# A selective-scan kernel with the preparation of six of its eight tiles placed inside the scan steps

## Chip, cores and metric

One core of a Trainium2 chip. The metric is the device time of one launch in microseconds (us).

## The reference

Two layers on x of 4 batches x 1024 positions x 256 channels. The first, a selective scan with 32 states per channel, is where the change is:

```python
A = -jnp.exp(A_log)
deltaBC = jnp.einsum('bld,od->blo', x, W_bc)          # x: normalised input
dt_r, Bm, Cm = deltaBC[..., :64], deltaBC[..., 64:96], deltaBC[..., 96:]
dt = jnp.einsum('blr,dr->bld', dt_r, W_dt)
delta = jax.nn.softplus(dt + b_dt[None, None, :])
# for each position t:
#   h = exp(delta_t * A) * h + (delta_t * x_t) * B_t
#   y_t = sum over states of h * C_t
y = y + x * D_param
```

The second layer is a small attention-like block with top-1 routing; it takes layer norm of x + y, convolves, projects, routes and adds.

## The kernel before

Every engine runs its own program; semaphores order them. The 1024 positions are eight tiles of 128 (`LT`), and for the scan 32 chunks of 32 (`CHUNKS`). There are three stages.

Preparation goes over the eight tiles. SP loads x; VectorE takes mean and variance (`statistics`, L1483), GpSimd the reciprocal root (`rstds`), VectorE normalises (L1507), TensorE transposes (L1233) and multiplies: dt_r (L1242), C (L1251), B (L1257), dt (L1268). ScalarE makes softplus as Abs, Exp, Ln (L1397 to L1403), VectorE adds it up into delta (L1557) and multiplies du (L1560). delta is transposed on TensorE (L1218). GpSimd makes x + D*xn (L1112, L1117), stored as `base`. delta, du and B are each split into three bf16 parts whose products give fp32 accuracy; the parts go through DRAM scratch (`delta_terms`, `du_terms`, `b_terms`; stores at L974 and L1027), since the scan needs them in another layout. All DMAs are issued by SP, in program order.

The scan goes over chunks; a chunk has eight steps, two halves (`SUBS`) of 16 positions times four groups (`GROUPS`) of 64 channels. All 128 partitions hold 4 batches x 32 states. In one step TensorE makes the input term B*du in one of two pairs of PSUM banks (L1329), adds the carry of the half before (L1336), then makes the arguments delta*A of the next chunk (L1286, `decay_args`), and in every second step contracts finished states with C (L1298, `contract`). ScalarE takes their exponentials (L1429), GpSimd computes the carry (L1180) and zeroes its decay (L1183), and VectorE scans 1024 elements per partition (L1606). For a step G, TensorE waits for scan G-2 (`scan_done >= G-1`) and for carry G; the carry waits for scan G-4; VectorE waits for the input term and the decay of G; ScalarE may be two PSUM banks behind the arguments. SP loads the parts of the chunk after next: `load_md` (12 DMAs, L991) once the arguments of the present chunk are finished, `load_mu` (6 DMAs, L998 and L1002) once its input terms are. y leaves PSUM through ScalarE (L1436) from one of two banks.

The first scan waits (L1588 to L1590) for the stores of the delta parts of all tiles, and the scan of step 4 for all of preparation (`p_done`).

The third stage, routing, starts as the last scan ends and runs over eight tiles again (`phase_f_*`).

## Time and profile before

| | us |
|---|---|
| median of 3 runs | 1005.86 (1002.33 to 1007.05) |
| profiled execution | 1001.59 |
| its span | 999.9 |

| engine | busy us (share of the span) |
|---|---|
| TensorE (PE) | 873.0 (87%) |
| VectorE (DVE) | 831.2 (83%) |
| ScalarE (ACT) | 460.2 (46%) |
| GpSimd (POOL) | 395.3 (40%) |

The mean granted clock of TensorE is 0.903 of its 2.4 GHz. PEld is its weight load, SPq the queue of SP, with the time in which it issues DMAs. A share over the whole span mixes three stages with different limits, so a view of one stage has to be read for each.

### The profile page before, as it was taken

Reading aid. Unit: us, or ns where it says so; the run is one execution under the profiler, and the core shown is the slowest. Engines: PE = TensorE matmul, PEld = TensorE weight load, DVE = VectorE, ACT = ScalarE, POOL = GpSimd, SP = SyncE. Lnnn points to the kernel's source line nnn. Section 1 sums busy time; section 2 is a strip of 40 time slices with the busy share of each in tenths; the row PEclk is TensorE's granted clock in tenths of the full one; section 3 lists DMA queues with packets and bytes.
Section 4 is the critical chain, followed back from the end, with each engine's and each line's share of the span. In section 5 each row is a group of like instructions: output and inputs, shape, how many; then the busy total and the mean of one; then the engine's idle time right before and its main releaser. Section 6 shows DMA issues by size and latency. Waiting matters only on the chain.

```text
span 999.9 us, 22490 instructions
## 1 busy us (share of the span) xinstructions
PE 873.0 (87%) x7440; PEld 670.1 (67%) x7440; DVE 831.2 (83%) x861; ACT 460.2 (46%) x798; POOL 395.3 (40%) x737
## 2 busy tenths in 40 slices
PE   5666666159999999999999999999999969899994
PEld 3434444148777777777777777777777747787873
DVE  6655765307999999999999999999999976899884
ACT  1554444533454545544545545454545334443631
POOL 6253333412333333333333333333333544456434
PEclk9776555556999999999999999999999989999997
DMA  9399999392222222222222221222222334210101
GB/s 329 84 150 162 165 170 171 88 163 82 64 65 78 61 76 67 59 77 66 61 79 63 68 72 61 76 64 61 79 64 64 110 106 138 56 51 22 43 22 63
DMA packets 206072, 89.93 MB, mean 90 GB/s; under 512 B 139220, under 2 KB 191956, under 8 KB 205268
## 3 DMA queue, kind: packets, MB, share of 16 engines
q1 hardware_dynamic: 206036, 89.49, 38.1%
q8 instruction: 18, 0.29, 0.1%
q14 instruction: 18, 0.15, 0.0%
HBM read 45.85 MB, written 43.61 MB: 89 GB/s over the span
## 4 chain that ended last, share of the span: by engine, by line
PE 65%; SPq 16%; DVE 8%; POOL 4%; issue 3%; ACT 2%; DMA 1%; ACTq 0%; DVEq 0%; POOLq 0%
PE psum L1329 23%; PE psum L1298 13%; PE psum L1286 11%; PE psum L1336 9%; SPq L974 7%; SPq L1027 6%; PE psum L458 5%; POOL arena L399 2%; DVE arena L1606 2%; SPq L991 1%; POOL arena L390 1%; SPq L968 1%; PE psum L527 1%; DVE delta_mov L706 1%; ACT arena L564 1%
## 5 line engine op out<-in xcount | busy, mean ns | idle before, releaser
L1606 DVE TENSOR_TENSOR_SCAN arena<-arena,psum 128x1024 f32<-128x1024 f32 x256 | 570.9, 2274 | 48.4 <-DMA delta_terms<-arena 29.4
L1429 ACT ACTIVATE arena<-psum 128x512 f32<-128x512 f32 x512 | 278.0, 595 | 303.4 <-PE psum L1286 299.7
L1329 PEld LDWEIGHTS psum<-du_mov,b_sta 96*128 96x128 bf16 x2048 | 206.8, 131 | 130.2 <-DVE arena L1606 127.2
L1329 PE MATMUL psum<-du_mov,b_sta 96*128 96x128 bf16 x2048 | 273.0, 315 | 13.2 <-DVE arena L1606 13.1
L1180 POOL TENSOR_TENSOR carry<-arena 128x64 f32<-128x64 f32 x252 | 110.7, 439 | 357.0 <-DVE arena L1606 270.4
L1286 PE MATMUL psum<-delta_mov,a_sta 96*128 96x128 bf16 x2048 | 163.5, 224 | 8.3 <-ACT arena L1429 8.3
L1286 PEld LDWEIGHTS psum<-delta_mov,a_sta 96*128 96x128 bf16 x2048 | 144.1, 110 | 11.2 <-ACT arena L1429 10.7
L1336 PE MATMUL psum<-carry,ident 128*128 128x32 f32 x1024 | 149.2, 270 | 0.0
L1336 PEld LDWEIGHTS psum<-carry,ident 128*128 128x128 f32 x1024 | 148.4, 206 | 0.0
L1298 PE MATMUL psum<-arena,c_sta 128*32 128x512 f32 x1024 | 148.0, 643 | 0.0
L458 PE MATMUL psum<-delta_mov,arena 128*128 128x256 f32 (+6 forms) x544 | 114.6, 368 | 8.0 <-ACT arena L579 7.9
L458 PEld LDWEIGHTS psum<-delta_mov,arena 128*128 128x128 f32 x544 | 88.8, 194 | 29.7 <-ACT arena L579 9.8
L1183 POOL TENSOR_TENSOR arena<-zeros 128x64 f32<-128x64 f32 x256 | 76.5, 299 | 20.0
L1242 PE MATMUL psum<-arena 128*64 128x512 f32 x32 | 29.4, 1074 | 50.0 <-ACT arena L1377 50.0
L1135 POOL TENSOR_TENSOR arena<-c_sta,arena 128x1024 f32<-128x1024 f32 x8 | 18.6, 2324 | 77.0 <-ACT arena L1416 77.0
L1242 PEld LDWEIGHTS psum<-arena 128*64 128x64 f32 x32 | 6.0, 218 | 63.0 <-ACT arena L1377 53.0
L399 POOL TENSOR_TENSOR arena<-arena 128x768 f32<-128x768 f32 (+2 forms) x24 | 36.0, 1502 | 9.2 <-DVE arena L755 6.6
L390 POOL TENSOR_TENSOR arena<-arena,delta_mov 128x1024 f32<-128x1024 f32 x8 | 15.5, 1932 | 60.5 <-DVE delta_mov L814 60.5
L1557 DVE SCALAR_TENSOR_TENSOR arena<-psum,arena 128x1024 f32<-128x1024 f32 x8 | 9.8, 1224 | 33.2 <-ACT arena L1403 33.2
L1488 DVE BATCH_NORM_STATS2 arena<-arena 128x6 f32<-128x256 f32 x32 | 11.2, 412 | 29.4 <-DMA arena<-in_L_attn_x 29.3
L527 PE MATMUL psum<-delta_mov,arena 128*128 128x256 f32 x128 | 30.9, 397 | 2.8 <-ACT arena L621 2.8
L701 DVE TENSOR_TENSOR arena<-arena,psum 128x512 f32<-128x512 f32 (+3 forms) x32 | 14.3, 481 | 21.3 <-ACT delta_mov L595 11.6
(142 smaller groups left out, 819.7 us busy)
## 6 DMA issues: line engine op xcount, KB each, us to landing
du_terms<-arena SPq DMA_DIRECT2D x48, 256.0 KB, 3.9
du_mov<-du_terms SPq DMA_DIRECT2D x128, 96.0 KB
y<-y_rows SPq DMA_DIRECT2D x32, 256.0 KB
b_terms<-delta_mov SPq DMA_DIRECT2D x6, 1024.0 KB, 10.6
delta_terms<-arena SPq DMA_DIRECT2D x48, 128.0 KB, 5.3
delta_mov<-delta_terms SPq DMA_DIRECT2D x128, 48.0 KB
b_sta<-b_terms SPq DMA_DIRECT2D x64, 96.0 KB
arena<-in_L_attn_x SPq DMA_DIRECT2D x8, 512.0 KB, 5.3
```

Source lines behind the costliest of these rows:

```text
L399: pool.tensor_tensor(o[:, 0:n], o[:, 0:n], arena[:, AV_TMP[m]:AV_TMP[m] + n], ALU.add)\
L458: mm = nc.tensor.matmul(psum[:, at:at + n], xc, w_all[:, h * WCOLS + col:h * WCOLS + col + n], start=(h == 0), stop=(h == 1))
L974: sp_.dma_start(dram(scratch_d, s * per_term + offset, *dims_), part(which)).then_inc(count, 16)
L1027: sp_.dma_start(dram(delta_terms_d, s * (B * L * D) + lt * (B * P * D) + h * (P * TC), (TC, P), (TC * D, B * P // TC), (1, TC)), dp_view(k ...
L1180: ins = pool.tensor_tensor(carry[:, g, :], seg[:, :, 0], before[:, :, TS - 1], ALU.mult)
L1183: pool.tensor_tensor(seg[:, :, 0], zeros[:, :], zeros[:, :], ALU.add)\
L1286: mm = nc.tensor.matmul(psum[:, (4 + u % 2) * BANK + i * P:(4 + u % 2) * BANK + (i + 1) * P], a_sta[0:ROWS, dg * P:(dg + 1) * P], sub(delt ...
L1298: mm = nc.tensor.matmul(psum[32 * j:32 * j + 32, (6 + k) * BANK:(6 + k) * BANK + TP * D], c_sta[k][:, (pi * 4 + j) * 32:(pi * 4 + j + 1) * ...
L1329: mm = nc.tensor.matmul(sub(psum, 0, P, o, (4, 4), (TS, GD // 2)), b_sta[k][0:ROWS, (s * 4 + tg) * P:(s * 4 + tg + 1) * P], sub(du_mov[k], ...
L1336: mm = nc.tensor.matmul(sub(psum, 0, P, (pair_bank + half) * BANK, (TS, GD // 2)), ident[:, :], carry[:, g, half * (GD // 2):(half + 1) * ...
L1429: nc.scalar.activation(sub(arena, 0, P, k * CHUNK_ELEMS + u * 16 * TS, (TS, 16), (D * TS, SUBS), (1, TS)), sub(psum, 0, P, (4 + u % 2) * B ...
L1606: nc.vector.tensor_tensor_scan(state[s][:, seg], decay[k][:, (s * D + g * GD) * TS:(s * D + (g + 1) * GD) * TS], psum[:, 2 * (step % 2) * ...
```

## The change

- Tiles 0 and 1 are prepared ahead of the scan. Tile p = 2 to 7 is prepared during the scan of tile p-2 (`EARLY` = 2): after a step's own work, each engine's program calls `p_piece(p, n, first)`, n counting the 32 steps of a tile, which issues the pieces given to that step. The stores and the load of x are placed in SP's program by chunk.
- delta is made transposed. W_bc's part for dt_r and W_dt are multiplied once into `w_eff`, and z = w_eff * xn^T gives channels by positions, so dt_r, its copy and the transposes of delta go; du is made transposed and is transposed back (`du_transposes`), and B comes out of one product with C and a transpose. The maximum with zero becomes a Relu on ScalarE; sums, differences and products move from VectorE to GpSimd, and the casts to ScalarE, for the streamed tiles.
- The arguments of a chunk run two steps later (`AHEAD` = 2), and the first half's decay has one buffer instead of two, which makes room for a tile in preparation.
- y uses PSUM bank 6 alone and one row buffer; bank 7 serves preparation.
- The zero fill of `b_terms` is issued by ScalarE.

The core of the diff, added lines only; what they replace is in the functions printed above:

```diff
+EARLY = 2
+CT = 4
...
+        HALF_CHUNK = D * TS
+        DECAY_AT = (0, (HALF_CHUNK, 2 * HALF_CHUNK))
+        STATE_AT = (3 * HALF_CHUNK, 4 * HALF_CHUNK)
+        def decay_at(k, s):
+            return DECAY_AT[1][k] if s else DECAY_AT[0]
...
+        x_t = [slot(20), slot(8)]
+        xn = [slot(21), slot(9)]
+        xnT = [slot(22), slot(10)]
+        sp = [slot(23), slot(11)]
+        delta = [slot(24), slot(16)]
+        duT = sp
+        du = xn
+        base_tmp = [slot(13), slot(14)]
+        def half_slot(i, h):
+            return slot(i)[:, h * 512:(h + 1) * 512].bitcast(BF16)
+        dparts = [[half_slot(20, 0), half_slot(20, 1), half_slot(23, 1)],
+                  [half_slot(17, 0), half_slot(17, 1), half_slot(18, 0)]]
+        uparts = [[half_slot(22, 0), half_slot(22, 1), half_slot(23, 0)],
+                  [half_slot(19, 0), half_slot(19, 1), half_slot(18, 1)]]
...
@@ block.sync @@
+            store_base(0, 0)
+            store_base(1, 1)
+            sp_.wait_ge(S["b_filled"], 16 * 3)
+            store_b(0, 0)
+            sp_.wait_ge(S["first_parts"], FIRST["dlo"])
+            store_delta(0, 0)
+            sp_.wait_ge(S["zeros_ready"], 3)
+            sp_.wait_ge(terms_stored[0], 16 * (TERMS + D_STORES))
+            load_md(0, 0)
+            sp_.wait_ge(S["first_parts"], FIRST["ulo"])
+            store_du(0, 0)
+            load_md(0, 1)
+            sp_.wait_ge(terms_stored[0], 16 * STORES)
+            load_mu(0, 0)
+            sp_.wait_ge(S["du1_zeroed"], 1)
+            load_mu(1, 1)
+            store_b(1, 1)
+            sp_.wait_ge(S["dlo_ready"], 1)
+            store_delta(1, 1)
+            sp_.wait_ge(S["ulo_ready"], 1)
+            store_du(1, 1)
...
+            def m_tile(lt, first, stream, last):
+                p = lt + EARLY
+                if stream:
+                    settle(sp_)
+                    sp_.wait_ge(terms_stored[0], 16 * STORES * (p - 1))
+                    load_x(p, 0)
+                for kk in range(CT):
+                    c, k = CT * lt + kk, kk % 2
+                    if not (last and kk >= 2):
                         settle(sp_)
                         sp_.wait_ge(S["args_ready"], (c + 1) * UNITS)
+                        if kk == 2 and first:
+                            sp_.wait_ge(terms_stored[1], 16 * STORES)
+                        elif kk == 2:
+                            settle(sp_)
+                            sp_.wait_ge(terms_stored[0], 16 * STORES * (lt + 1))
+                        load_md(lt + (kk + 2) // CT, (kk + 2) % CT)
+                    if last and kk == 2:
+                        settle(sp_)
                         sp_.wait_ge(S["args_ready"], (c + 1) * UNITS)
                         load_f_weights(sp_)
+                    if last and kk == 3:
+                        settle(sp_)
                         sp_.wait_ge(S["b_ready"], c * STEPS)
+                        settle(sp_)
+                        sp_.wait_ge(S["y_stored"], 16 * 2 * CT)
                         f_load(sp_, 0, 0)
                         f_load(sp_, 1, 1)
+                    if stream and kk == 1:
+                        store_base(p, 0)
+                    if stream and kk == 3:
+                        settle(sp_)
+                        sp_.wait_ge(S["dlo_ready"], p)
+                        store_delta(p, 0)
+                    if not (first and kk == 0):
+                        store_y(c - 1)
+                    if stream and kk == 2:
+                        store_b(p, 0)
+                    if stream and kk == 3:
+                        settle(sp_)
+                        sp_.wait_ge(S["ulo_ready"], p)
+                        store_du(p, 0)
+                    if not (last and kk >= 2):
                         settle(sp_)
                         sp_.wait_ge(S["b_ready"], (c + 1) * STEPS)
                         load_mu(c + 2, k)
...
@@ block.gpsimd @@
+            rstds(0, 0)
+            rstds(1, 1)
+            for p in range(EARLY):
+                pool.wait_ge(S["first_xn"], p + 1)
+                base_product(p, p, base_tmp[p])
+                base_sum(p, p, base_tmp[p])
+            pool.memset(du_mov[1][:, :].bitcast(F32), 0.0).then_inc(S["du1_zeroed"], 1)
+            b_rest(0, 0)
+            b_low(0, 0)
             for k in range(2):
                 pool.memset(c_sta[k][:, :], 0.0).then_inc(S["c_sta_zeroed"], 1)
+            b_rest(1, 1)
+            b_low(1, 1)
+            delta_sum(1, 1)
+            du_product(1, 1)
+            delta_rest(1, 1)
+            delta_low(1, 1)
+            du_rest(1, 1)
+            du_low(1, 1)
             pool.wait_ge(S["c_sta_zeroed"], 2)
             pool.wait_ge(S["own_made"], 3)
...
+            def p_piece(p, n, first):
+                if n == 3:
+                    if first:
+                        pool.wait_ge(S["first_xn"], 2)
+                    else:
+                        pool.wait_ge(S["xn_ready"], p - 2)
+                    rstds(p, 0)
+                if n == 6:
+                    pool.wait_ge(S["xn_ready"], p - 1)
+                    pool.wait_ge(S["duT_psum"], 2 * p)
+                    pool.wait_ge(terms_stored[0], 16 * STORES * (p - 1))
+                    base_product(p, 0, sp[0])
+                if n == 8:
+                    base_sum(p, 0, sp[0])
+                if n == 18:
+                    b_rest(p, 0)
+                if n == 19:
+                    b_low(p, 0)
+                if n == 20:
+                    delta_sum(p, 0)
+                if n == 21:
+                    du_product(p, 0)
+                if n == 23:
+                    delta_rest(p, 0)
+                if n == 25:
+                    delta_low(p, 0)
+                if n == 27:
+                    du_rest(p, 0)
+                if n == 29:
+                    du_low(p, 0)
...
@@ block.tensor @@
+            def z_mul(k, half, at, o, n, h):
+                return nc.tensor.matmul(bank(at)[:, o:o + n], w_eff[:, h * D + half * P:h * D + (half + 1) * P],
+                                        xnT[k][:, h * BANK + o:h * BANK + o + n], start=(h == 0), stop=(h == 1))
+            def cb_products(k, at):
+                for o, w in ((0, R + N), (P, R)):
                     for b in range(B):
                         for h in range(2):
+                            mm = nc.tensor.matmul(bank(at)[N * b:N * b + N, o:o + P],
+                                                  w_bcT[:, h * P + w:h * P + w + N],
+                                                  xnT[k][:, h * BANK + b * P:h * BANK + (b + 1) * P],
                                                   start=(h == 0), stop=(h == 1))
+                mm.then_inc(S["bc_psum"], 1)
+            def p_piece(p, n, first):
+                if n == 6:
+                    pe.wait_ge(S["duT_taken"], 2 * p)
+                    pe.wait_ge(S["xn_ready"], p - 1)
+                    xn_transposes(0, 0, 7)
+                if n == 7:
+                    pe.wait_ge(S["xnT_ready"], 2 * p + 1)
+                    xn_transposes(0, 1, 7)
+                if 8 <= n < 16:
+                    half, i = (n - 8) // 4, n % 4
+                    if i == 0 and half == 0:
+                        pe.wait_ge(S["xnT_ready"], 2 * p + 2)
+                    if i == 0 and half == 1:
+                        pe.wait_ge(S["z_taken"], 2 * p + 1)
+                    mm = z_mul(0, half, 7, (i // 2) * D, D, i % 2)
+                    if i == 3:
+                        mm.then_inc(S["z_psum"], 1)
+                if n == 16:
+                    pe.wait_ge(S["z_taken"], 2 * p + 2)
+                    cb_products(0, 7)
+                if n == 17:
+                    b_transpose(p, 0, 7)
+                if n == 23:
+                    pe.wait_ge(S["bhi_ready"], p + 1)
+                    pe.wait_ge(S["du_ready"], p)
+                    du_transposes(0, 0, 7)
+                if n == 24:
+                    pe.wait_ge(S["duT_taken"], 2 * p + 1)
+                    du_transposes(0, 1, 7)
+            AHEAD = 2
...
+                            if step < AHEAD:
+                                for u in range((step + STEPS - AHEAD) * UNITS_PER_STEP,
+                                               (step + STEPS - AHEAD + 1) * UNITS_PER_STEP):
+                                    mm = decay_args(c, k, u, True)
+                            elif not (last and kk == 3):
+                                if step == AHEAD:
+                                    pe.wait_ge(md_loaded[1 - k], 16 * MD_LOADS * (2 * lt + (kk + 1) // 2 + 1))
+                                for u in range((step - AHEAD) * UNITS_PER_STEP, (step - AHEAD + 1) * UNITS_PER_STEP):
                                     mm = decay_args(c + 1, 1 - k, u, True)
+                            if stream:
+                                p_piece(lt + EARLY, kk * STEPS + step, first)
...
@@ block.scalar @@
+            act.wait_ge(S["zeros_ready"], 1)
+            row_elems = TERMS * B * L * P // P // 3
+            for i in range(3):
+                act.dma_start(dram(b_terms_d, i * P * row_elems, (row_elems, P), (1, row_elems)),
+                              delta_mov[0][:, 0:row_elems]).then_inc(S["b_filled"], 16)
...
+            def take_z(p, k, half, at):
+                act.wait_ge(S["z_psum"], 2 * p + half + 1)
+                cols = slice(half * BANK, (half + 1) * BANK)
+                nc.scalar.activation(sp[k][:, cols], bank(at), ACT.Abs, bias=bdt[:, half:half + 1])\
+                    .then_inc(S["z_abs"], 1)
+                nc.scalar.activation(delta[k][:, cols], bank(at), ACT.Relu, bias=bdt[:, half:half + 1])\
+                    .then_inc(S["z_taken"], 1)
+            def exp_part(p, k):
+                act.wait_ge(S["z_abs"], 2 * p + 2)
+                nc.scalar.activation(sp[k], sp[k], ACT.Exp, scale=-1.0).then_inc(S["sp_exp"], 1)
+            def ln_part(p, k):
+                act.wait_ge(S["sp_exp"], p + 1)
+                nc.scalar.activation(sp[k], sp[k], ACT.Ln, bias=1.0).then_inc(S["sp_ln"], 1)
...
+            def p_piece(p, n, first):
+                if n == 5:
+                    act.wait_ge(S["ulo_ready"], p - 1)
+                    if first:
+                        act.wait_ge(S["first_parts"], FIRST["ulo"])
+                    normalise(p)
+                if n == 6:
+                    act.wait_ge(terms_stored[0], 16 * STORES * (p - 1))
+                    take_xnT(p, 0, 0, 7)
+                if n == 7:
+                    take_xnT(p, 0, 1, 7)
+                if n == 11:
+                    act.wait_ge(S["base_ready"], p + 1)
+                    act.wait_ge(S["dlo_ready"], p - 1)
+                    take_z(p, 0, 0, 7)
+                if n == 15:
+                    take_z(p, 0, 1, 7)
+                if n == 16:
+                    exp_part(p, 0)
+                    take_cb(p, 0, 7)
+                if n == 17:
+                    act.wait_ge(S["blo_ready"], p)
+                    act.wait_ge(terms_stored[0], 16 * STORES * (p - 1))
+                    take_b(p, 0, 7)
+                if n == 18:
+                    b_middle(p, 0)
+                    ln_part(p, 0)
+                if n == 22:
+                    act.wait_ge(base_stored[0], 16 * p)
+                    delta_high(p, 0)
+                if n == 23:
+                    take_du(p, 0, 0, 7)
+                if n == 24:
+                    take_du(p, 0, 1, 7)
+                    delta_middle(p, 0)
+                if n == 26:
+                    du_high(p, 0)
+                if n == 28:
+                    du_middle(p, 0)
...
@@ block.vector @@
+            def p_piece(p, n, first):
+                if n == 2:
+                    dve.wait_ge(x_loaded[0], 16 * p)
+                    statistics(p, 0)
+                if n == 4:
+                    dve.wait_ge(S["rstd_ready"], p + 1)
+                    if not first:
+                        dve.wait_ge(S["xn_ready"], p - 2)
+                    nc.vector.scalar_tensor_tensor(out=shift, in0=mv[0][:, 0:7:2], scalar=-1.0, in1=rstd[0],
+                                                   op0=ALU.mult, op1=ALU.mult).then_inc(S["shift_ready"], 1)
```

## Rows read from the trace of the kernel before

**Rows 1.** Source view: count, duration ns min/median/max, first and last start

```profile
L1606 DVE TENSOR_TENSOR_SCAN arena<-arena,psum x256: 2260/2264/2289, 222.8 to 810.4; 128x1024 f32<-128x1024 f32 x128
```

**Rows 2.** Windows view, scan: busy us by engine, clock, DMA share, GB/s

```profile
222.80:812.70 589.90, 585.03 (x6033) 454.12 (x6033) 570.83 (x257) 282.59 (x524) 214.37 (x619) 0.98 0.24 72
```

**Rows 3.** Timeline, mid-scan: start, duration, engine, line, operation, idle before

```profile
503.02 18.04 DVE L1606 TENSOR_TENSOR_SCAN arena<-arena,psum 128x1024 f32<-128x1024 f32 x8 [0.23 <-PE psum L1336]
...
503.10 1.04 PE L1329 MATMUL psum<-du_mov,b_sta 96*128 96x128 bf16 x8
...
503.94 0.57 PE L1336 MATMUL psum<-carry,ident 128*128 128x32 f32 x4
...
504.77 1.09 ACT L1429 ACTIVATE arena<-psum 128x512 f32<-128x512 f32 x2 [0.60 <-PE psum L1286]
...
505.45 0.43 POOL L1180 TENSOR_TENSOR carry<-arena 128x64 f32<-128x64 f32 x1 [1.68 <-DVE arena L1606]
...
507.64 1.04 PE L1329 MATMUL psum<-du_mov,b_sta 96*128 96x128 bf16 x8
```

**Rows 4.** Timeline of SP's queue in preparation, issue times of groups of DMAs

```profile
11.64 10.59 SPq L960 DMA_DIRECT2D a_terms<-arena  x6
...
71.98 2.96 SPq L968 DMA_DIRECT2D a_sta<-a_terms  x4
75.47 7.41 SPq L1027 DMA_DIRECT2D delta_terms<-arena  x6
82.99 5.17 SPq L974 DMA_DIRECT2D du_terms<-arena  x6
...
178.00 7.81 SPq L991 DMA_DIRECT2D delta_mov<-delta_terms  x12
```

**Rows 5.** Timeline of SP's queue in the middle of the scan

```profile
500.09 1.81 SPq L998 DMA_DIRECT2D du_mov<-du_terms  x4
502.08 1.56 SPq L1002 DMA_DIRECT2D b_sta<-b_terms  x2
503.93 8.88 SPq L991 DMA_DIRECT2D delta_mov<-delta_terms  x12
```

**Rows 6.** DMA view: issues by destination, KB each, median us to landing

```profile
arena<-in_L_attn_x SPq DMA_DIRECT2D x8, 512.0 KB, 5.3
```

**Rows 7.** Timeline, TensorE: narrow products (preparation), transposes, fp32 products (routing)

```profile
54.25 0.70 PE L1251 MATMUL psum<-arena 128*32 128x128 f32 x16
...
888.35 1.04 PE L451 MATMUL psum<-ident,arena 128*128 128x128 f32 x8
889.31 3.69 PE L458 MATMUL psum<-delta_mov,arena 128*128 128x256 f32 x16
```

**Rows 8.** Timeline, routing stage: statistics of a tile, then the power

```profile
812.63 1.38 DVE L671 BATCH_NORM_STATS2 delta_mov<-arena 128x6 f32<-128x256 f32 x4
...
814.71 1.02 POOL L384 TENSOR_TENSOR delta_mov<-delta_mov 128x4 f32<-128x4 f32 x1 [4.46 <-DVE delta_mov L679]
```

**Rows 9.** Timeline: long operations of GpSimd and ScalarE, and one normalisation

```profile
156.75 2.12 POOL L1138 TENSOR_TENSOR arena<-arena 128x1024 bf16<-128x1024 f32 x1 [1.16 <-ACT arena L1418]
...
158.83 2.35 POOL L1112 TENSOR_TENSOR arena<-arena 128x1024 f32<-128x1024 f32 x1
...
160.95 1.28 ACT L1403 ACT_TABLE_LOAD   x1
...
162.24 1.06 ACT L1403 ACTIVATE arena<-arena 128x1024 f32<-128x1024 f32 x1
...
826.85 2.06 ACT L564 ACTIVATE arena<-arena,delta_mov 128x256 f32<-128x256 f32 x4
```

**Rows 10.** Windows view: the first scans, and around a pause of TensorE

```profile
227.80:240.80 13.00, 13.00 (x80) 11.14 (x78) 9.15 (x4) 4.34 (x8) 3.69 (x12) 0.50 0.17 57
816.00:820.00 4.00, 1.16 (x8) 0.86 (x8) 3.25 (x13) 3.25 (x6) 0.52 (x1) 0.87 0.26 52
824.00:828.00 4.00, 4.00 (x18) 3.04 (x18) 0.00 (x0) 1.65 (x4) 0.88 (x1) 0.77 0.73 218
```

838 lines of the change are left out of this document (378 added, 460 removed).

## The prediction

> **What bounds the kernel now.** I read the source view of the scan first [rows 1]: 256 instructions of one length, 2.26 us, the first at 222.8, the last ended at 812.7. So preparation of all eight tiles takes 222.8 us, the scan 589.9 and the routing stage the rest of the span, 187.2. Busy time within the scan [rows 2] puts TensorE at 585, VectorE at 571. Then comes one stretch of the timeline in the middle of the scan [rows 3]. Eight scans run without a gap in 18.04 us, after 0.23 us of waiting for L1336: 2.284 us a step. TensorE is not slack beside this. From one product B at L1329 (503.10) to the next but one (507.64) is 4.54 us, and two scans are 4.53 us; within it each operation starts as the one before ends. So both engines are full: work added to either lengthens a step, and a stall on either is kept. ScalarE and GpSimd have time over (283 and 214 us busy of 590, [rows 2]), but they have results due inside a step.
>
> I call S the start of B of a step. By [rows 3] the carry is wanted at S+0.8, and the exponentials end at S+2.8 (504.77 + 1.09 - 503.10).
>
> **Before the first scan.** The new kernel prepares two tiles instead of eight; SP's queue sets the end. Its stores of the split A are issued from 11.6 [rows 4]; the fill of b_terms, now on ScalarE's queue, still moves the same 6.3 MB beside them, so I take them as landed at 24 (bounds 18 and 28). Sixteen loads of a_sta, four in 2.96: 36. Tile 0's base store lands 5.3 after its issue, as x does [rows 6], and the split of delta, which writes over that tile, follows (four operations over 1024 columns, 1.06 each as Ln [rows 9]: 4): 45. Six delta stores 7.4, landed 4 later; twelve loads of delta_mov 7.8; du stores 5.2; twelve more loads 7.8: 77 [rows 4]. du_mov and b_sta 3.4 [rows 5], landing 4, gaps 0.8, B and carry at half clock 2.9: first scan at 88 (80 to 98) instead of 222.8. That is 135 us gained.
>
> Behind it SP issues load_mu(1) 3.4, b 5.2, delta 7.4, du 5.2, and only then load_x(2), landing 5.3 later: x of tile 2 is there at 108. VectorE asks for it in its third step, at 88 + 3 x 3.25 = 98, and cannot scan on.
>
> **A tile with preparation in it: what moves with it.** TensorE gets, per tile, 16 fp32 transposes at 0.12 (eight in 0.96, from 888.35 to 889.31): 1.9; eight z products of 256 columns, 3.53 (889.31 to 892.84); 16 small C and B products, twice the 0.70 of the eight at L1251, less a tail: 1.3; one transpose 0.1. Together 6.9 [rows 7], on a full engine. VectorE gets statistics, 2.0 (812.63 to 814.63), and the 0.2 of shift [rows 8].
>
> SP gets the stores, 5.2 + 7.4 + 5.2 + 1.7. In each tile's last chunk they stand in one line with the next load_x. From S of step 25: arguments finished 1.8, load_md 8.9, delta stores 7.4, y 0.7 as one of those loads, du stores 5.2, load_mu 3.4, gaps 0.6, x landing 5.3 [rows 4 to 6] = 33.3. The code puts it so: load_x(p) waits for the stores of p-1 and stands behind load_mu. VectorE asks for x behind step 2 of the next tile, which without waits is S25 + 9 x 2.284 + 3.9 = 24.5 later (28.2 with those of the carry below). So scans stop for 5 to 9 us in every streamed tile, queued behind `wait_ge(x_loaded[0])`. Bounds of the landing: 4 (an idle queue, the first x of the run) and 10 (the 128 x 16 x 6 pieces of 64 B of the delta stores still draining).
>
> After x: statistics 2.0, a scan 2.3, 0.1, then step 5 begins: 4.4. Twenty steps to step 25: 45.7. Onto these come the 6.9 of matmul work and the waits inside steps:
> - Step 6: normalise on ScalarE starts after the exponentials of step 5 and takes 2.06 [rows 9]; TensorE wants its transposes 0.4 earlier. GpSimd's base_product (2.35) then comes before the carry of step 7: 1.5.
> - Step 18: Ln needs a table load of 1.28 and the exponentials another, since here both loaded [rows 9]; with Ln 1.06 the arguments of step 20 wait 1.3.
> - Steps 22 to 30: a cast on ScalarE of 1.06, as Ln (till S+3.9), a GpSimd operation of 2.1 (S+6.1), the next carry 0.43: S+6.6 where S+5.4 is wanted. Less the 0.5 of a transpose group: 0.7 for step 24. The later three (3.7 together) lie inside the SP leg and cost nothing there, except in the last streamed tile.
> Sum 3.9, bounds 0 and 7 (the trace has no such queueing; the nearest is GpSimd waiting for ScalarE's cast in preparation, and I take the middle since each wait follows from durations in rows).
> - The clock. TensorE is idle for about 7 us at each x wait. In [rows 10] a stretch of 4 us with 1.16 busy ended with the clock falling to half, and in the 4 us around 825, after TensorE took up steady work at 822.9, it averaged 0.77; beside the first scans it stayed at half through 13 us of unbroken work. I take 2.0 per tile (0 to 5).
>
> The y bank costs nothing: its copy has from the contraction of step 3 to that of step 5. If ScalarE were late there, the contraction would wait; its lead is 2 us. The folded weight removes the dtr product and its copy from preparation, which is off SP's line.
>
> Streamed tile: 33.3 + 4.4 + 45.7 + 6.9 + 3.9 + 2.0 = 96.2, where a plain one is 73.1.
>
> **The sum.** S25 of tile 0 at 108.3 + 4.4 + 45.7 + 12.8 + 2 (half clock at the start) = 173.2. x of the next at 206.5. Four more tiles: 591.3. To the last S25: + 62.9 = 654.2. Seven steps and the three carry waits 19.7; 64 plain steps 146.2; last scan's end 2.1: 822.2. Routing stage as before, 187.2: 1009.4. Around the span lie 1.7 (1001.59 against 999.9): 1011. That is 9 us above the profiled execution's own time, and 5 above the median 1005.86 of the runs (the profiled one was 4 below it). So the 135 us come back: 138 in six tiles of 23 each, and some 10 at the first x.
>
> **Where the skill speaks.** The Trainium skill, page "ScalarE: Activation LUTs", section "Table sets: the hidden batching unit", says exp and ln share one set, so that ln after exp needs no second load. The trace disagrees: 1.28 us at L1403 ahead of Ln, and as much ahead of Exp. By the page step 18 would cost nothing and the sum be 8 us lower. On the clock, the Trainium skill, page "TensorE: Matmul & The Clock Gate", section "HAM oscillation — how this bites in real kernels", says that a wait for a DMA in every loop turn makes every turn start cold. The trace agrees for one wait [rows 10]; with that in each tile it is the second rival.
>
> **Rivals.**
> 1. The added work costs only itself. GpSimd, ScalarE and the clock have room; x still comes late. For it: steps are regular to 1%, and leads may absorb the waits. Against: results are due within one step. 1011 - 6 x 5.9 - 3.7 = 972. If x is in time from tile 1 on as well (SP's issue far faster than in preparation), each tile adds only 9.1: 88 + 589.9 + 9.8 + 54.6 + 187.2 + 1.7 = 931.
> 2. Slower. TensorE stays at half clock after every x wait. A step is 3.25 us then (four scans in 13 us at 0.50, [rows 10]). [...] 17 us of it is 5.2 steps x 0.97 = 5.1, and with the doubled transposes 6: 4 more per tile, 1035. A landing of 10 instead of 5.3 adds up to 24 more.
> 3. The change doesn't do what it says: the first scan is not early, since step 4 also waits for the stores of tile 1. Those land near 106, x at 108, so it is hidden; if the first scans came at 120, all shifts by 32: 1043.
>
> **Chances.** Forecast 0.42, rival 1 0.34 (972: 0.26; 931: 0.08), rival 2 0.20, rival 3 0.04. The likeliest case by itself spans 990 to 1025 (first scan, waits). Range: 948 to 1046, with the upper bounds of landing and the middle between the two forms of rival 1. A difference of 0.5% (5 us) is about what a measurement can tell from no change. Faster by over that, below 1000.8: rival 1 and a quarter of the forecast, 0.44. Within: 0.17. Slower: 0.39.
>
> **What would show it.** In the profile after: first scan at 88; VectorE waiting for the x load at step 2 in six tiles, 5 to 10 us each; clock below 1 right after; GpSimd's carry late for L1336 by 1 us behind base_product and the splits; SP busy in one line in each tile's last chunk; streamed tiles of 96 us, the last two of 73. No wait for x, or full clock throughout, and the number is wrong towards fast; scan steps of 3.25 us for long stretches, towards slow.

## The result, and the profile after

The changed kernel takes 1032.0 us (median of 4 runs, 1025.0 to 1035.3) against 1004.1 for the kernel before (999.96 to 1007.05): ratio 1.027, 95% interval 1.020 to 1.034. It is slower. The profiled execution took 1035.3 us, its span is 1033.4. The forecast was 1011 in a range of 948 to 1046, so the range held it and the forecast was 21 us low. Runs over 1.5% above the fastest of the same kernel are left out below: one of ten of the kernel with both edits, and two of four of the one with only TensorE's loop written out.

The page of the changed kernel: the span, the busy time by engine, TensorE's granted clock in 40 slices (9 is full), and the packets of the instruction queue.

```profile
span 1033.4 us, 21756 instructions
...
PE 886.0 (86%) x7468; PEld 677.4 (66%) x7468; DVE 763.5 (74%) x772; ACT 490.3 (47%) x883; POOL 456.7 (44%) x779
...
PEclk9655699899969896999699969899999998999998
...
q8 instruction: 69, 1.13, 0.5%
```

TensorE's clock is no longer full in the middle of the run; before it was, there (0.98 over the whole scan, first steps included, [rows 2]). The last row counts fetches of instructions: 69 packets, where the same row of the kernel before has 18.

VectorE's timeline in tile 0 (start, duration, what ended the idle time):

```profile
78.90 2.29 DVE L1736 TENSOR_TENSOR_SCAN arena<-arena,psum 128x1024 f32<-128x1024 f32 x1 [29.25 <-PE psum L1401]
...
98.61 1.41 DVE L1642 BATCH_NORM_STATS2 small<-arena 128x6 f32<-128x256 f32 x4 [10.95 <-DMA arena<-in_L_attn_x]
```

The first scan begins at 78.9 instead of 222.8 [rows 1]. After three steps VectorE stands 10.95 us for x. In tile 1 it stands again:

```profile
200.37 1.41 DVE L1642 BATCH_NORM_STATS2 small<-arena 128x6 f32<-128x256 f32 x4 [4.38 <-DMA arena<-in_L_attn_x]
```

SyncE's queue ahead of that second wait, from the arguments of step 25 on, which answers to the sum of [rows 4, 5]:

```profile
169.91 4.04 SPq L959 DMA_DIRECT2D delta_mov<-delta_terms  x12
174.06 7.32 SPq L944 DMA_DIRECT2D delta_terms<-arena  x6
...
183.57 6.34 SPq L951 DMA_DIRECT2D du_terms<-arena  x6
...
194.31 0.42 SPq L900 DMA_DIRECT2D arena<-in_L_attn_x  x1
```

The line is the forecast one, from delta_mov's load to delta's stores, du's stores and, last, x. Step 25 begins at 168.0, and x is there at 200.4: 32.4 us for a predicted 33.3. That the sum fits so well is partly luck: inside it the load of delta_mov was issued in 4.0 us (8.9 forecast), and du's stores in 6.3 (5.2), x's landing in 6.1 (5.3) and the gaps made up for most of it.

Then the forecast stops holding. In tiles 2 to 5 nobody waits for x. All engines at the seam between tiles 1 and 2:

```profile
283.06 1.13 PE L1333 MATMUL psum<-arena,c_sta 128*32 128x512 f32 x8
...
284.25 0.43 POOL L1204 TENSOR_TENSOR carry<-arena 128x64 f32<-128x64 f32 x1 [0.36 <-ACT arena L1547]
...
289.44 1.89 PE L1394 MATMUL psum<-du_mov,b_sta 96*128 96x128 bf16 x8 [5.25 <-issue]
...
292.23 2.29 DVE L1736 TENSOR_TENSOR_SCAN arena<-arena,psum 128x1024 f32<-128x1024 f32 x1 [6.66 <-PE psum L1401]
...
293.32 0.40 SPq L900 DMA_DIRECT2D arena<-in_L_attn_x  x1
```

TensorE's contraction at 283.06 belongs to step 31, and GpSimd has run ahead with the carries of the next steps, up to 284.25. TensorE starts B of step 0 (L1394) at 289.44, after 5.25 us released by "issue": no semaphore event explains it. VectorE waits 6.66 us behind it, and x, issued at 293.3, then comes in time for step 2. The same stop stands at 394.1 (5.10), 497.1 (5.00) and 600.3 (5.61). It is absent before tile 1, entered from straight code, and before tile 6, behind the loop. It is where the loop (`Fori`) over tiles 1 to 5 jumps back. TensorE's clock there, in stretches of 4 us (busy time of each engine, then PEclk, DMA share, GB/s):

```profile
core 0: us, PE busy (x) PEld busy (x) DVE busy (x) ACT busy (x) POOL busy (x), PEclk, DMA share, GB/s
284.00:288.00 4.00, 0.19 (x4) 0.00 (x0) 1.57 (x1) 0.03 (x1) 0.73 (x2) 0.79 0.86 235
288.00:292.00 4.00, 2.56 (x14) 2.56 (x15) 0.00 (x0) 0.00 (x0) 0.00 (x0) 0.50 0.77 217
292.00:296.00 4.00, 4.00 (x29) 3.86 (x26) 2.90 (x2) 1.34 (x3) 0.00 (x0) 0.50 0.56 177
296.00:300.00 4.00, 4.00 (x21) 2.28 (x19) 1.67 (x1) 0.83 (x2) 0.73 (x2) 0.51 0.33 101
300.00:304.00 4.00, 4.00 (x44) 2.94 (x44) 3.58 (x5) 2.49 (x5) 0.00 (x0) 1.00 0.13 37
...
308.00:312.00 4.00, 4.00 (x26) 2.75 (x24) 3.17 (x3) 1.83 (x5) 0.01 (x1) 0.50 0.12 46
```

The clock falls to 0.5 in the stop (the lower of its two levels, 1.2 of 2.4 GHz), stays there until 300 though TensorE is busy from 289.4 on, and is at 0.5 again from 308, after TensorE had waited 1.6 us for a carry. Behind the four jumps TensorE worked at half clock for some 10, 18, 18 and 10 us.

From the waits view (us in total, times, longest):

```profile
DVE arena L1736 <- PE psum L1401: 180.2, 98, 29.3
...
PE psum L1401 <- POOL carry L1204: 45.0, 33, 11.2
```

TensorE's longest stops for a carry stand where VectorE waits for x: 11.2 us in tile 0, 6.1 in tile 1, where the next carry stands on GpSimd behind the power for 1/std.

From statistics to statistics a tile lasts 101.8 us, then 102.3, 104.9, 102.9 and 103.0: 103.0 on average, where 96.2 was forecast.

### The profile page after: what moved, and what is told of

It reads as the page before. It is cut to its first block, busy times and chain, and to the rows that moved or that the text cites. A ratio compares the mean times of both kernels' runs of the same rounds, so it can differ in the third digit from the quotient of the medians.

```text
span 1033.4 us, 21756 instructions
## 1 busy us (share of the span) xinstructions
PE 886.0 (86%) x7468; PEld 677.4 (66%) x7468; DVE 763.5 (74%) x772; ACT 490.3 (47%) x883; POOL 456.7 (44%) x779
## 4 chain that ended last, share of the span: by engine, by line
PE 51%; issue 18%; DVE 9%; POOL 7%; ACT 6%; SPq 6%; DMA 2%; ACTq 0%; POOLq 0%; DVEq 0%
PE psum L1394 16%; PE psum L1333 9%; PE psum L1321 8%; PE psum L1401 8%; PE psum L427 5%; DVE arena L1736 3%; PE psum L1254 2%; POOL arena L368 2%; POOL carry L1204 2%; ACT arena L1547 1%; SPq L944 1%; POOL arena L359 1%; SPq L923 1%; PE psum L496 1%; ACT arena L1456 1%
## 5 line engine op out<-in xcount | busy, mean ns | idle before, releaser
L1394 PEld LDWEIGHTS psum<-du_mov,b_sta 96*128 96x128 bf16 x2048 | 226.4, 139 | 160.0 <-issue 89.4
L1394 PE MATMUL psum<-du_mov,b_sta 96*128 96x128 bf16 x2048 | 294.8, 333 | 29.5 <-issue 21.0
L1401 PE MATMUL psum<-carry,ident 128*128 128x32 f32 x1024 | 159.5, 281 | 45.0 <-POOL carry L1204 45.0
L1321 PE MATMUL psum<-delta_mov,a_sta 96*128 96x128 bf16 x2048 | 173.5, 232 | 17.5 <-ACT arena L1547 10.7
L1321 PEld LDWEIGHTS psum<-delta_mov,a_sta 96*128 96x128 bf16 x2048 | 153.0, 115 | 21.6 <-ACT arena L1547 14.2
L1333 PE MATMUL psum<-arena,c_sta 128*32 128x512 f32 x1024 | 157.2, 684 | 0.0
L427 PEld LDWEIGHTS psum<-delta_mov,arena 128*128 128x128 f32 x544 | 88.6, 194 | 29.6 <-ACT arena L548 9.5
L1254 PE MATMUL psum<-arena,w_eff 128*128 128x256 f32 (+1 forms) x112 | 43.2, 478 | 2.1 <-ACT arena L1462 2.1
L1333 PEld LDWEIGHTS psum<-arena,c_sta 128*32 128x32 f32 x1024 | 21.0, 112 | 21.3 <-issue 13.3
L1077 POOL TENSOR_TENSOR arena<-arena,d_bc 128x1024 f32<-128x1024 f32 x8 | 18.9, 2358 | 35.5 <-ACT arena L1456 34.6
L670 DVE TENSOR_TENSOR arena<-arena,psum 128x512 f32<-128x512 f32 (+3 forms) x32 | 14.3, 481 | 21.6 <-ACT delta_mov L564 11.9
L496 PEld LDWEIGHTS psum<-delta_mov,arena 128*128 128x128 f32 x128 | 25.5, 201 | 7.2 <-ACT arena L590 3.4
```

The costliest lines, as they stand in the source:

```text
L427: mm = nc.tensor.matmul(psum[:, at:at + n], xc, w_all[:, h * WCOLS + col:h * WCOLS + col + n], start=(h == 0), stop=(h == 1))
L496: mm = nc.tensor.matmul(psum[:, 6 * BANK + b * D:6 * BANK + (b + 1) * D], fgT[:, (h * B + b) * P:(h * B + b + 1) * P], w_out[:, h * D:(h + ...
L1254: return nc.tensor.matmul(bank(at)[:, o:o + n], w_eff[:, h * D + half * P:h * D + (half + 1) * P], xnT[k][:, h * BANK + o:h * BANK + o + n ...
L1321: mm = nc.tensor.matmul(psum[:, (4 + u % 2) * BANK + i * P:(4 + u % 2) * BANK + (i + 1) * P], a_sta[0:ROWS, dg * P:(dg + 1) * P], sub(delt ...
L1333: mm = nc.tensor.matmul(psum[32 * j:32 * j + 32, 6 * BANK:6 * BANK + TP * D], c_sta[k][:, (pi * 4 + j) * 32:(pi * 4 + j + 1) * 32], sub(ar ...
L1394: mm = nc.tensor.matmul(sub(psum, 0, P, o, (4, 4), (TS, GD // 2)), b_sta[k][0:ROWS, (s * 4 + tg) * P:(s * 4 + tg + 1) * P], sub(du_mov[k], ...
```

## The experiments

Theory B is the prediction's: SyncE's line to x and the waits inside the steps set a tile. Theory A: the jump of the loop costs by itself. Theory D came after the first results: short stops of TensorE cost twice, by the half clock behind them. Experiments 1 to 4, 5 to 8 and 9 to 11 each shared a chip and its runs of the kernel before; across chips I compare ratios to the kernel before. A difference between two of these kernels is uncertain by 6 to 8 us, from the intervals of their ratios. Numbers 4, 5 and 7 build on number 3 (both edits), 6 on 5, and 9 to 11 on 6.

**1 to 3. The loop written out, x ahead, both.**

```diff
-            with eng.Fori(1, LT - EARLY) as it:
-                body(it, False, True, False)
+            for lt in range(1, LT - EARLY):
+                body(lt, False, True, False)
```

> The changed kernel with the loop over tiles 1 to 5 written out on every engine, nothing else. Theory A (the jump back costs by itself): in the changed kernel TensorE stands for 5.0 to 5.6 us before step 0 of tiles 2 to 5, released by nothing that the profile shows, and runs at half its clock for most of the next 20 us. Written out, these four idles vanish and the waits for x come in their place, as in tile 1 (4.4 us); tiles 2 to 5 then last 102 us as tile 1 does instead of 105, and the kernel takes about 1020 us. Theory B (SyncE's line to x sets the tile's length, and the idle at the loop's end only stands where the wait for x would): the tiles keep their 105 us and the time stays within 3 us of 1032. Theory C (the idle is a wait for data, a DMA that lands late, not for the jump): the 5 us before step 0 stay where they are, loop or no loop.

Measured 1020.6 us (1011.5 to 1024.3), ratio 1.019 (1.016 to 1.022): 11 us less than the changed kernel by the medians, 8 by the ratios. VectorE, tile 2:

```profile
296.19 1.41 DVE L1642 BATCH_NORM_STATS2 small<-arena 128x6 f32<-128x256 f32 x4 [3.97 <-DMA arena<-in_L_attn_x]
```

No stop at the jump; the wait for x, 3.7 to 5.0 us in each tile, stands in its place. A tile lasts 98.3 us on average (98.62 to 590.17 for five). That is below the 102 I had given it, but this is the profiled execution, 1011.5 us, the fastest of the four and 9 below their median; spread over five tiles the median stands for about 100. Behind the wait for x TensorE works at half clock for nearly 8 us in tile 2, and for over 10 in tiles 1 and 4, much as behind the stop at the jump. The stop is the jump's, as theory A has it, and theories B and C fall; the time gained is small, because a wait for x of almost the same length stands where the stop was.

The second edit, x ahead (SyncE's own loop is written out with it):

```diff
+            load_x(2, 0)
...
-                if stream:
+                if not last:
                     settle(sp_)
-                    sp_.wait_ge(terms_stored[0], 16 * STORES * (p - 1))
-                    load_x(p, 0)
+                    sp_.wait_ge(terms_stored[0], 16 * 2 * TERMS * (p - 1))
...
+                        if more:
+                            settle(sp_)
+                            sp_.wait_ge(d_stored, 16 * D_STORES * p)
+                            load_x(p + 1, 0)
```

> The changed kernel, loops kept on all engines but SyncE, whose own loop is written out; the next streamed tile's x is loaded by SyncE in the last chunk of the tile before, as soon as the delta terms have left that buffer (they now count on a semaphore of their own) and after the du stores are issued; x of tile 2 is loaded ahead of the stores of tile 1. Theory B: the wait for x (15.3 us in two tiles of the changed kernel, and as much as 4.5 in each of the others had the jump not stood there) is what lengthens the tiles: the time falls by 15 us or more, to 1017 or less. Theory A: the waits of tiles 0 and 1 go (15 us at most, less what the stores of tile 1 then make tile 0 wait for elsewhere, 5 or so), and tiles 2 to 5 keep 105 us because the 5 us before step 0 stay: 1018 to 1027.

Measured 1020.9 (1018.8 to 1022.8), ratio 1.018 (1.015 to 1.021). The statistics of tile 0 begin at 87.5 instead of 98.6: the whole wait of 10.95 is gone. Some of that is lost again: from the statistics of tile 1 to those of tile 2 it takes 107.7 us (102.3 in the changed kernel), with a mean granted clock of 0.83. From tile 2 to 5 a tile still lasts 102.5 us, and the stop at the jump is still there (5.14 us at 277.65). So in those tiles an earlier x gives about 1 us, as A has it.

The third kernel has both.

> Both edits: every engine's loop written out and x loaded ahead. Theory A: neither idle is left; a tile lasts 102 less 4.4, about 98 us, and the kernel takes 985 to 1000 us, so that the edits together give 30 to 45 us where each alone gives 8 to 15. Theory B alone (the loop costs nothing): the time is that of x loaded ahead with the loop kept. If tiles still last over 101 us, a third thing sets them: the waits inside the steps, for which the carry on GpSimd is the first candidate.

Measured 991.8 (984.6 to 997.0, nine runs), ratio 0.988 (0.985 to 0.991): 1.2% faster than the kernel before. By the ratios the two edits give 8 and 9 us alone, each hardly clear of the noise, and 39 together. Two stops at one place hid each other: whoever removes one meets the other. A tile lasts 95.4 us.

**8 and 12. Whose jump.** Only TensorE's loop written out, then TensorE's and SyncE's.

```diff
-            tiles(pe, m_tile)
+            for lt in range(LT):
+                m_tile(lt, lt == 0, lt < LT - EARLY, lt == LT - 1)
```

> The changed kernel with the loop over tiles 1 to 5 written out on TensorE alone; the others keep theirs. Theory A1 (it is TensorE's own jump, its loop body being fetched anew): the 5 us stops before step 0 of tiles 2 to 5 are gone and the time is that of all loops written out, 1018 to 1023. Theory A2 (another engine is late after its jump, GpSimd or VectorE, and TensorE's stop only follows): the stops stay and so do 1032 us. Both in part: 1024 to 1030.

Measured 1020.4 and 1030.0, the latter profiled; the kernel before beside it 1004.6. (The 1032.9 of the next expectation is the median with the two runs that are left out here, 1035.8 and 1036.6.) Two runs 10 us apart don't tell A1's time from A2's; the mechanism, read in the trace, is A1's. TensorE at the seam between tiles 1 and 2 (contraction of step 31, then B of step 0), and VectorE behind step 2:

```profile
283.96 1.07 PE L1333 MATMUL psum<-arena,c_sta 128*32 128x512 f32 x8
284.96 1.05 PE L1394 MATMUL psum<-du_mov,b_sta 96*128 96x128 bf16 x8
```

```profile
299.84 1.41 DVE L1643 BATCH_NORM_STATS2 small<-arena 128x6 f32<-128x256 f32 x4 [6.54 <-DMA arena<-in_L_attn_x]
```

TensorE runs through this seam and the three behind it without a stop, so the stop was its own jump's; waits for x of 5.1 to 6.5 us took its place. I had tied the place of the stop and the total together, and they come apart.

> The changed kernel with the loop over tiles written out on TensorE and SyncE, kept on the other three engines. With TensorE's alone written out its stop at the jump went, and waits for x of 5.1 to 6.5 us stood in its place, at the same total of 1032.9; with all written out those waits were 4.0 to 5.0 and the total 1020.6. Theory A3 (the rest is SyncE's own jump, which there put 0.8 us between its last load and the one of x, against 0.1): the waits for x shorten to 4 to 5 us and the time comes to 1018 to 1025. Theory A4 (the jumps of ScalarE, GpSimd and VectorE delay the chain to x): the waits stay over 5 us and the time at 1028 to 1035.

Measured 1014.2 (1012.1 to 1016.7), ratio 1.010 (1.003 to 1.018); the waits for x are 4.0 to 5.0, and between SyncE's last load and that of x lie 0.11 us instead of 0.84. By the waits this is theory A3, SyncE's own jump delays x; the time lies below A3's range of 1018 to 1025. The loops of the three other engines cost nothing that can be told from this (all written out: ratio 1.016 to 1.022, an interval that overlaps).

**4. What GpSimd's queue costs.** Six of GpSimd's eight long pieces cut to 8 columns:

```diff
+            def cut(p, t):
+                return t[:, 0:8] if long_p(p) else t
...
-                pool.tensor_tensor(delta[k], delta[k], sp[k], ALU.add).then_inc(S["delta_ready"], 1)
+                pool.tensor_tensor(cut(p, delta[k]), cut(p, delta[k]), cut(p, sp[k]), ALU.add).then_inc(S["delta_ready"], 1)
...
```

> As the kernel with both edits, and six of the eight long operations of GpSimd in each streamed tile (base product and sum, delta's sum, du's product, the first residuals of delta and du) work on 8 columns instead of 1024, so the output is not the reference's; the two lowest parts are still made in full. It prices the queueing of the carry behind them. By the prediction's sum the carry waits are 2.2 us a tile: the time falls by about 13 us against the kernel with both edits. Rival: the gaps seen before steps 6, 21, 22, 24 and 26 of the changed kernel (2.2, 2.6, 2.2, 1.8 and 1.6 us) are all GpSimd's, about 6 to 8 us a tile: it falls by 35 to 50 us. If it falls by less than 6 us, the gaps are TensorE's own, from the matmuls put into the steps.

Measured 983.7 (975.5 to 988.4), ratio 0.978 (0.974 to 0.983), 8 us below the one with both edits beside it, give or take 6: 1.4 a tile. The rival's 35 to 50 fall; the prediction's 13 can't be told from this, nor can a gain under 6. GpSimd's length is not what makes most of the gaps.

**5 to 7. The stops of TensorE.** In the kernel with both edits, two stops of TensorE in tile 3:

```profile
379.39 0.63 PE L1409 MATMUL psum<-carry,ident 128*128 128x32 f32 x4 [2.07 <-POOL carry L1212]
```

```profile
426.88 0.89 PE L1329 MATMUL psum<-delta_mov,a_sta 96*128 96x128 bf16 x8 [1.39 <-ACT arena L1555]
```

ScalarE ahead of the second (L1486 is Ln, L1555 the exponentials):

```profile
422.56 1.28 ACT L1486 ACT_TABLE_LOAD   x1
423.86 1.06 ACT L1486 ACTIVATE arena<-arena 128x1024 f32<-128x1024 f32 x1
424.93 1.28 ACT L1555 ACT_TABLE_LOAD   x1
```

VectorE's longest gap behind each:

```profile
387.82 4.46 DVE L1744 TENSOR_TENSOR_SCAN arena<-arena,psum 128x1024 f32<-128x1024 f32 x2 [2.76 <-PE psum L1409]
...
434.83 2.29 DVE L1744 TENSOR_TENSOR_SCAN arena<-arena,psum 128x1024 f32<-128x1024 f32 x1 [2.95 <-PE psum L1409]
```

Stretches of 4 us, columns as above:

```profile
376.00:380.00 4.00, 1.93 (x19) 1.38 (x16) 3.88 (x11) 0.82 (x2) 2.01 (x4) 1.00 0.40 122
380.00:384.00 4.00, 4.00 (x33) 3.45 (x34) 3.57 (x3) 1.96 (x4) 1.08 (x4) 0.57 0.20 69
384.00:388.00 4.00, 4.00 (x29) 2.69 (x21) 1.24 (x2) 2.17 (x5) 1.75 (x1) 0.58 0.00 0
388.00:392.00 4.00, 4.00 (x43) 2.98 (x41) 4.00 (x2) 3.13 (x6) 3.84 (x8) 1.00 0.19 55
...
424.00:428.00 4.00, 2.52 (x29) 2.17 (x26) 3.81 (x2) 3.97 (x6) 2.93 (x3) 1.00 0.00 0
428.00:432.00 4.00, 4.00 (x26) 2.28 (x24) 2.29 (x1) 1.86 (x4) 3.78 (x6) 0.54 0.28 53
432.00:436.00 4.00, 4.00 (x28) 3.86 (x25) 1.17 (x1) 0.75 (x2) 0.00 (x0) 0.50 0.47 66
436.00:440.00 4.00, 4.00 (x27) 3.49 (x28) 3.03 (x2) 2.63 (x5) 2.59 (x3) 0.50 0.17 51
440.00:444.00 4.00, 4.00 (x34) 2.51 (x27) 1.15 (x2) 0.92 (x3) 1.43 (x5) 0.75 0.32 95
```

Here each stop, of 2.1 and of 1.4 us, is followed by half clock, 7 us long behind the first (0.57, 0.58) and 14 behind the second, and by gaps of 2.8 and 3.0 us of VectorE, in which TensorE is busy without pause at half clock.

That is one tile. The same stop in tile 1 of the same kernel, and the clock behind it:

```profile
237.39 0.88 PE L1329 MATMUL psum<-delta_mov,a_sta 96*128 96x128 bf16 x8 [1.45 <-ACT arena L1555]
...
236.00:240.00 4.00, 2.52 (x32) 2.24 (x36) 2.70 (x3) 3.51 (x7) 3.92 (x4) 1.00 0.04 6
240.00:244.00 4.00, 4.00 (x43) 3.12 (x44) 3.45 (x2) 2.19 (x5) 2.32 (x5) 1.00 0.47 88
```

The clock stays full, as it does behind this stop in tiles 0 and 4 (146.1, 524.4); in tiles 2 and 5 it is at half for some 3 and 7 us. So theory D holds on average and not for each stop, and no run here separates what decides it.

```diff
-                if n == 3:
+                if n == 4:
                     if first:
                         pool.wait_ge(S["first_xn"], 2)
...
```

> The kernel with loops written out and x loaded ahead, and one piece on GpSimd moved by a step: the power that gives 1/std, which there stands between the carries of steps 3 and 4 and waits 5.3 us for VectorE's statistics, goes behind the carry of step 4. In the trace of that kernel the carry of step 4 comes late for it, TensorE stands for 2.1 us, and its granted clock falls to 0.5 for the next 7 us, in which VectorE waits 2.8 us before step 5. Theory D (a short stop of TensorE costs twice, by the clock after it): 4 to 5 us a streamed tile go though the stop is 2.1 us long: 992 falls by 20 to 30 us. Rival (only the stop itself counts, the gap at step 5 has another cause): by 2 us a tile, 12 in all. Second rival (the statistics' own 2 us are hidden by nothing, TensorE waits for VectorE there anyway): by under 5 us.

Measured 990.8 (983.8 to 991.5), ratio 0.985 (0.979 to 0.991), the same as without. The carry is in time now and the stop is still there, released by VectorE:

```profile
381.72 1.14 PE L1402 MATMUL psum<-du_mov,b_sta 96*128 96x128 bf16 x8 [2.26 <-DVE arena L1744]
```

VectorE owes TensorE its buffer and is 2.0 us late by the statistics themselves: the second rival. The carry had only been the last of two to arrive.

The next kernel also moves the pieces of steps 20 to 29 by one, and loads x ahead of du's stores:

```diff
-                if n == 20:
+                if n == 21:
                     delta_sum(p, 0)
...
```

> As the one before, and every piece of the step numbers 20 to 29 goes one step later on GpSimd, TensorE and ScalarE, so that delta's sum, which waits on GpSimd for the logarithm, stands behind the carry of step 21 and no longer ahead of it; SyncE loads x of the next tile ahead of the du stores. In the kernel with both edits TensorE stood 1.5 us there (424 to 428) and its clock was 0.5 for 15 us, with gaps of 1.7, 3.0, 1.0 and 2.9 us before the next steps. Theory D: another 4 to 6 us a tile go, 25 to 35 us in all against the kernel before it. Rival: the new place only moves the queue, the carries of steps 24 to 26 come late in its stead: within 5 us of the kernel before it. It could also be slower, by up to 3 us a tile, if x then lands later than step 2.

Measured 983.9 (979.2 to 986.4), ratio 0.979 (0.973 to 0.985): 7 below the one before it, on the same chip, though the two intervals overlap, and the fastest here with the whole computation. Its own theory falls, 25 to 35 were expected; the rival's 5 is near. The stop at step 21 stays, 1.45 us, and TensorE's arguments (L1329) end it, released by ScalarE:

```profile
423.67 0.89 PE L1329 MATMUL psum<-delta_mov,a_sta 96*128 96x128 bf16 x8 [1.45 <-ACT arena L1555]
```

They wait for exponentials that stand behind Ln and its table loads, not for the carry.

```diff
-                nc.scalar.activation(sp[k], sp[k], ACT.Ln, bias=1.0).then_inc(S["sp_ln"], 1)
+                if k == 0 and (not isinstance(p, int) or p >= EARLY):
+                    nc.scalar.activation(sp[k], sp[k], ACT.Identity).then_inc(S["sp_ln"], 1)
...
```

> The kernel with loops written out and x loaded ahead, and ScalarE's logarithm of a streamed tile replaced by a copy of the same 128x1024 elements, so the output is not the reference's; the two loads of ScalarE's tables, 1.28 us each in the trace, go with it. The prediction put 1.3 us a tile on this place: 8 us over six tiles. Theory D: the late carry of step 21 hangs on it (delta's sum waits for the logarithm ahead of that carry), and with it the stop of TensorE and the 15 us of half clock: 4 to 6 us a tile, 25 to 35 us in all. Rival (the table loads are hidden behind ScalarE's idle time, a third of the stretch): under 4 us.

Measured 968.4 (964.6 to 970.7), ratio 0.966 (0.961 to 0.971); against 0.988 with the logarithm that is 22.7 us, 3.8 a tile (2.8 to 4.8 by the intervals), for 2.56 us of table loads and a piece of the same length as before. TensorE's stop of 1.4 us at step 21 is gone in every streamed tile. The mechanism is the place where ScalarE makes TensorE stop; the carry, which the expectation names, had no part in it, as the kernel before this showed.

**9 to 11. The rest of the sum**, built on the kernel with carries first.

```diff
                 if n == 2:
                     dve.wait_ge(x_loaded[0], 16 * p)
-                    statistics(p, 0)
+                    for b in range(2):
+                        nc.vector.bn_stats(stats[0][:, 6 * b:6 * b + 6], x_t[0][:, b * D:(b + 1) * D])
+                if n == 3:
+                    statistics(p, 0, 2)
```

> The kernel with the carries first (loops written out, x ahead), and the statistics of a streamed tile in two halves: two of VectorE's four reductions behind the scan of step 2, the other two and the rest behind that of step 3. In the kernel before it TensorE stood 1.6 to 2.5 us for VectorE there and its clock was 0.5 for the next 7 us, in which the gaps before steps 5 to 7 add 2.5 to 4.4 us. Theory D (a stop of some length lowers the clock): halves of 0.8 and 1.2 us are too short for it, and 2 to 4 us a tile go, 12 to 24 in all, to 960 to 972. Rival (VectorE's work adds up wherever it stands, the half clock costs little since VectorE is late anyway): within 4 us of the kernel before it, 984.

Measured 991.8 (988.3 to 993.0), ratio 0.990 (0.987 to 0.993) against 0.979 without the split: not faster, rather slower. VectorE's stop shrank to 0.35 us, but 1/std comes later for the split, and the carry behind it too; 1.78 us of stop is back one step on, and the half clock with it:

```profile
379.28 1.06 PE L1409 MATMUL psum<-carry,ident 128*128 128x32 f32 x4 [1.78 <-POOL carry L1212]
```

> As the kernel with the carries first, with the statistics of streamed tiles on 8 columns a batch instead of 256, and the logarithm replaced by a copy as above; the output is not the reference's. Of what stops TensorE in a streamed tile little is left, its added matmuls all are. The prediction has 73.1 us for a tile without preparation and 6.9 for the matmuls. Theory D: the granted clock is over 0.98 in the streamed tiles and a tile lasts 80 to 84 us against 94, so the kernel takes 915 to 930. Rival (the clock falls for another reason, the denser matmuls themselves or the transfers): the clock stays near 0.95 and a tile lasts 87 to 89: 950 to 965.

```diff
-                    ins = nc.vector.bn_stats(stats[k][:, 6 * b:6 * b + 6], x_t[k][:, b * D:(b + 1) * D])
+                    w = 8 if not isinstance(p, int) or p >= EARLY else D
+                    ins = nc.vector.bn_stats(stats[k][:, 6 * b:6 * b + 6], x_t[k][:, b * D:b * D + w])
```

Measured 942.3 (940.1 to 946.4), ratio 0.942 (0.938 to 0.946): 37 us below. The stretch from 200 to 300, first of the kernel it is built on, then of this one:

```profile
200.00:300.00 100.00, 94.50 (x876) 71.78 (x869) 77.31 (x45) 53.72 (x97) 47.53 (x88) 0.90 0.38 93
```

```profile
200.00:300.00 100.00, 95.39 (x970) 72.83 (x969) 83.92 (x49) 56.23 (x104) 49.00 (x98) 1.00 0.40 99
```

The added matmuls don't lower the clock: it is 1.00 against 0.90, with one stop of 1.2 us a tile left and the others at most 0.8. The time lies between the two ranges. Three of five tiles last 85.8 us, the first 93.1 and the last 87.4, not 80 to 84. Beyond 73.1 + 6.9, GpSimd's late carries make 3.9 us of stops in such a tile (1.23, 0.32, 0.80, 0.75, 0.76), and the statistics one of 0.6; 1.3 of the 85.8 us are left over. The prediction named these carries and had them larger, 1.5 at step 7 and 4.4 for the four behind steps 22 to 30.

```diff
+                if at == 7 and k == 0 and n == D:
+                    n = 8
                 return nc.tensor.matmul(bank(at)[:, o:o + n], w_eff[:, h * D + half * P:h * D + (half + 1) * P],
...
```

> As the kernel with the carries first, and the eight matmuls of z in each streamed tile work on 8 columns instead of 256, so the output is not the reference's. The prediction prices z at 3.53 us a tile with TensorE full: 21 us for six tiles, 984 falls to 963. Rival (VectorE, 77% busy there, or the stops set the pace, and the matmuls fill stops): under 8 us. If the gaps of 1.05 us before every second step from 8 to 16 vanish, they were z's, 5 of them a tile: 5.3 us a tile or 32 in all.

Measured 961.5 (953.3 to 963.8), ratio 0.958 (0.952 to 0.963), 21.6 us below by the ratios: 3.6 a tile (2.3 to 4.9 by the intervals), for 3.53 predicted. VectorE's gaps, first with z whole, then with z small:

```profile
395.43 4.47 DVE L1744 TENSOR_TENSOR_SCAN arena<-arena,psum 128x1024 f32<-128x1024 f32 x2 [1.05 <-PE psum L1409]
400.99 4.48 DVE L1744 TENSOR_TENSOR_SCAN arena<-arena,psum 128x1024 f32<-128x1024 f32 x2 [1.09 <-PE psum L1409]
```

```profile
383.39 4.46 DVE L1746 TENSOR_TENSOR_SCAN arena<-arena,psum 128x1024 f32<-128x1024 f32 x2 [0.45 <-PE psum L1411]
388.29 4.46 DVE L1746 TENSOR_TENSOR_SCAN arena<-arena,psum 128x1024 f32<-128x1024 f32 x2 [0.43 <-PE psum L1411]
```

The regular gap of 1.05 us before every second step falls to 0.45: both engines were full, and z was paid. How closely 3.6 meets 3.53 is luck. Two steps took 5.58 us with z whole (B at 393.91 to B at 399.49, at full clock) and 4.91 with it small (291.14 to 296.05), which over eight steps is 2.7 us a tile; the eight columns left still take 0.2 to 0.27 us a step, where the whole piece takes 0.49 to 0.58, 4.3 us a tile. The 0.9 us between 2.7 and 3.6 lie within the noise.

## Why the prediction was off, step by step

- **What bounds the kernel** held: TensorE and VectorE both full, work added to either is kept. The z products show it: 3.53 predicted, 3.6 measured for most of their length, with an interval of 2.3 to 4.9.
- **First scan.** 88 predicted, 78.9 measured, a microsecond below its bounds of 80 to 98. The wait for x in tile 0 was put at 10 and is 10.95; statistics at 98.6 instead of 108.3. This made the forecast 9.7 us too high.
- **SyncE's line of 33.3 us** held ahead of tile 1 (32.4, by errors that cancel in part), the wait there nearly (4.4, for 5 to 9 forecast). In tiles 2 to 5 it hid behind something else.
- **What failed first: the jump had no term.** The streamed tile was summed as if tiles 1 to 5 were straight code. The kernel before has such a loop, too, and its turns cost nothing visible in [rows 1, 3]; I took the same for the changed one, whose body holds twice as many chunks and the pieces of preparation in each. Its jump stops TensorE for 5.0 to 5.6 us, four times, and delays SyncE's next load; in tiles 2 to 5 the forecast wait for x is hidden behind it. A tile was 6.4 us over the 96.6 forecast (96.2, tile 0's start spread over five). Written out, five tiles fell from 103.0 us each to 98.3, but these are two profiled executions 24 us apart, where the medians of the two kernels are 11 apart. Brought to the medians a tile takes about 102.3 and 100.1: the jump is worth about 2 us a tile, not 4.7.
- **What failed second, and weighs more: waits inside steps and clock**, 3.9 + 2.0, were mis-sized. Without jump and with the wait for x, the tile of 98.3 leaves 98.3 - 33.3 - 4.4 - 45.7 - 6.9 = 8.0, and about 10 at the median of that kernel, 3.5 more than the 3.9 + 2.0 and the share of tile 0's start. Where x is in time the clock still falls: the place of the statistics (2.0 on VectorE, with the power behind them on GpSimd) and Ln (2.56 of table loads on ScalarE) each stop TensorE for 1.4 to 2.6 us a tile, and between none and 15 us of half clock follow. I charged step 18 with 1.3; it costs 3.8 where nothing hides it.
- **The sum.** Actual less forecast span: -9.7 (start), +31.8 (five tiles), +2.3 (last two and the tail of tile 5), -0.4 (routing): 24.0, from 1009.4 to 1033.4. The errors have opposite signs; that the range held the result is partly luck, and the forecast looks better than its steps.
- **The rivals.** The first, 972, fell: results due within one step were indeed late. The second, at half clock after each x wait, is near in time (1035) and right in half its mechanism: half clock came, for 10 to 18 us where it put 17, but in four of six tiles behind the jump, not behind x. The third fell, the first scan is early.
- **The Trainium skill**, page "ScalarE: Activation LUTs", section "Table sets: the hidden batching unit", has exp and ln in one set. The trace of the kernel with both edits disagrees again, 1.28 us ahead of L1486 and ahead of L1555 in each streamed tile, and the run without Ln prices the two at 3.8 us a tile. The Trainium skill, page "TensorE: Matmul & The Clock Gate", section "HAM oscillation — how this bites in real kernels", has every turn of a loop with a DMA wait start cold. The trace agrees: half clock follows the wait for x in tiles 0 and 1, and in all six tiles of the kernel with loops written out. It also follows the jump, which is no such wait, and many, not all, of the waits of 1.4 to 2.6 us for VectorE, ScalarE and GpSimd.

What stays open: why the jump takes 5 us. The instruction queue moves 3 packets (0.05 MB) in a stretch of 8 to 14 us around a jump and 7 to 9 packets per 100 us of the changed loop; in the kernel before it moves none from 400 to 700. A turn there has 387 matmuls and 385 weight loads, a turn of the changed loop 837 and 833, by the windows view of one turn each. So a long body is fetched anew at each turn, and a short one isn't. Fetching by itself stops nothing: with all loops written out the queue moves 6 to 8 packets per 100 us, and TensorE has no stop there. That its stop is the fetch behind a jump, beside du's stores (217 to 235 GB/s in those stretches), is argued, not shown. A loop with a shorter body and the same pieces would have told, and wasn't run. Nor was a version that keeps the whole computation without the stops of statistics and Ln. Open, too, is why the same stop brings half clock in one tile and none in the next.

The Trainium skill, page "Runtime: NRT & Kernel Launch", section "Instruction fetch mechanics", bears on this: fetching ahead is sequential, and a taken branch whose target is no longer held stalls until it is fetched. It gives TensorE room for 2048 instructions. The trace agrees in direction: 772 matmuls and weight loads a turn without a stop, 1670 with one, where registers and semaphores come on top; whether those bring it over 2048 no run here shows. I had not weighed this section of the Trainium skill, and it speaks against the change.

## What to carry to other kernels

When work moves into a hardware loop, the loop's turn is a step to be priced like any other: compare the length of its body with one whose turns cost nothing, and look at the seams first when the result is in. Where one place has two causes to wait, removing either gives little and both give the sum; so judge an edit there only with its partner. On two full engines, count a stop of TensorE with the half clock that may follow: here a stop of 1.4 us, with the table loads that made it, was worth nearly 4 on average over six tiles. And compare two kernels by their medians: two profiled executions can differ by twice as much, since the clock does not fall behind the same stops in each.

## What the runs showed of the hardware that I had not expected

A jump back of TensorE stopped it for 5.0 to 5.6 us in this loop and for no visible time in the shorter one of the kernel before. Short stops of TensorE were followed by half clock for 3 to 15 us in most cases and by none in others. Over the traces of the changed kernel and its variants, from 130 us on, the clock fell within 5 us behind 37 of 66 stops at step 21 (1.3 to 1.5 us), and behind 42 of 44 of 1.4 to 3.5 us for GpSimd or VectorE; one of 1.64 us at 378.4, in the kernel with carries first, left it full. In the kernel with stops of 0.3 to 1.2 us it stayed at 1.00 from 200 to 400, and fell for some 3 us behind one of 1.2 us at 449. The time of a kernel moves with it: with loops written out, 1011.5 us at a mean granted clock of 0.911 and 1024.3 at 0.897. And the sum of it: 143.9 us came off the time before the first scan, while the scan grew from 589.9 to 767.7, by 177.8. Preparation beside work on two full engines cost more than it had by itself. Without the jump and the waits for x it no longer did: with both edits the scan lasts 721.6 us, 131.7 more than before.
